# A four-layer graph network on one core: three moves of order, and the second graph's attention in the last one's buffers

## The chip, the core and the metric

The kernel runs on one core of a Trainium2 chip. The time is the device time of one execution, in microseconds. A run that is profiled is one more execution of the same program. In what follows PE is TensorE (its weight loads are shown apart as PEld), DVE is VectorE, ACT is ScalarE, POOL is GpSimd, and SP is the engine whose queue issues most of the DMAs. Every engine works through its own instructions strictly in the order in which they are written; they meet only at semaphores.

## The reference

There are 16 graphs of 1024 nodes with 128 features each, `x` (16, 1024, 128), and a matrix of integers `adj` (16, 1024, 1024) that holds 0 and 1. Four layers stand on a residual stream, and each reads a normalized copy of it:

```python
h = relu(layernorm(x));  x = x + L0(h, adj)    # degree-weighted mean, 2 batch norms
h = relu(layernorm(x));  x = x + L1(h, adj)    # graph attention
h = relu(layernorm(x));  x = x + L2(h, adj)    # attention with products as scores
h = relu(layernorm(x));  x = x + L3(h, adj)    # graph attention, elu

# L0
w = masked_row_softmax(adj.T)                  # adj is 0/1: division by the degree
region = batch_norm(w @ features @ kernel_1 + bias_1)      # over all 16 graphs
people = batch_norm(w.T @ region @ kernel_2 + bias_2)      # over all 16 graphs
# L1, and L3 with elu on the result
Wh = h @ W
e = leaky_relu(Wh @ a_src [rows] + Wh @ a_dst [columns])
out = softmax(where(adj == 0, -inf, e)) @ Wh
# L2
e = leaky_relu(sum_d hidden[i, d] * hidden[j, d] * a_0[d])  # adj == 1 only
out = softmax(where(adj == 1, e, -9e15)) @ hidden
```

Both batch norms of layer 0 need sums over all graphs, so the kernel has three stages one behind the other.

## The kernel before

Nodes are held as 8 tiles (or columns) of 128. The order of the work is written out by hand for each engine; no planner stands between.

**Stage a** (to about 252 us) walks over the 16 graphs, 8 columns c each. TensorE turns a column of `adj` (8 transposes, L360), multiplies it with the normalized x in two half-precision parts (16 matmuls, L372 to L376, into one of three PSUM banks, `psW`), and three columns later adds up sums (L335). ScalarE keeps the turned mask (`maskT`, L316) and divides column c-1 by the degree (`divide`, L296); `keep_whT` (L305) stands after column 3 and, for the column group of the graph that ended, in the next graph. VectorE has for each column the function `tail(b, c)` (L243, L245, L246: the degree and its reciprocal, which let ScalarE divide) and `rest(b, c-1)` (L251: the lower half of the quotient, which waits for ScalarE's divide and gives the PSUM bank free). I call these four instructions a pair. Between the pairs VectorE makes the next graph's normalized x: `stats` (L212), `moments` (L217, L219), then GpSimd takes a power (`rs_a`, L185), then `shifts` (L223), `normed` twice (L228), `high` (L233) and `low` (L237). TensorE waits with the next graph's first product until `low` is done. TensorE also waits, before the product of column n, until `rest` of column n-3 is done, since that is in the same PSUM bank.

**Stage b** (about 252 to 421 us) is the second half of layer 0. TensorE makes `rows(b)` (L710, 16 matmuls in the trace) and `product(b)` (L721, 32 matmuls); VectorE makes the row's parts in `graph(b)` (L620 to L636), of which L630 lets TensorE start `rows(b+1)` and L636 lets it start `product(b)`. At its start, once, `later_weights_dve` and `later_weights_pe` (L536 to L554, L533) prepare weights of stage c.

**Stage c** (421 us to the end) holds layers 1 to 3, called A, B and C, as a pipeline: the turn i works on A's attention of graph i, on B's of graph i-1 and on C's of graph i-2. In A and C the masked weights (`weights`, L1010 on VectorE, 8 tiles a graph) are the product of a row factor `row_`, a column factor `least_` and the mask from the `ring_` buffers, and TensorE's `weigh` (L1703, and L1716 in `weigh_half` where the first half of the columns is done for all tiles at once) multiplies them with `hP_`. Before that stand `columns` (L971, L974: the `peak`), `highest` on TensorE (L1653), `exponents` (L979 to L983), `rows` (L1639), then ScalarE's `exps` (L1376, L1377), `row_power` (L1384) and `factors` (L1403). In B TensorE turns the normalized values (`turn_h`, L1630 in the trace), they are split (ScalarE `g_hi`, L1445; VectorE `g_lo`, L1051), and three matmuls a tile (L1674 to L1676) make the scores. `shares` (L1032, L1034) is the reciprocal of the sums behind a weighing, `shifts` (L957) the end of a layer norm.

Of the kernel before, what the change touches and what calls it, by code (L numbers as in the profile page):

```python
# [6 lines left out]
def gnn_stack_kernel(nc, x_in, adj, k1, b1, g1, be1, k2, b2, g2, be2,  # L7
# [12 lines left out]
    P = 128  # L20
# [19 lines left out]
    with ctx:  # L40
# [84 lines left out]
        with ExitStack() as a_ctx:  # L125
# [42 lines left out]
            with nc.allow_non_contiguous_dma("small weight vectors"), nc.Block() as block:  # L168
# [38 lines left out]
                def _(dve):  # L207
# [348 lines left out]
        with ExitStack() as b_ctx:  # L556
# [16 lines left out]
            with nc.Block() as block:  # L573
# [43 lines left out]
                def _(dve):  # L617
# [86 lines left out]
                def _(pe):  # L704
# [43 lines left out]
        with ExitStack() as c_ctx:  # L748
# [37 lines left out]
            def home(x, b):  # L786

                return "A" if x == "C" and b == B - 1 else x

# [53 lines left out]
            with nc.Block() as block:  # L843
                @block.sync
                def _(sp):
# [13 lines left out]
                    def load_row(x, b):  # L859
# [3 lines left out]
                        if b > 0:  # L863
                            sp.wait_ge(S[x, "wts"], b * T)
                        sp.dma_start(row_e[x][:, :], row_dram[x][n % 2].rearrange("t p -> (t p)").partition_broadcast(P)) \
# [16 lines left out]
                    for i in range(-1, B + 2):  # L882
# [20 lines left out]
                        if 0 <= i + 1 < B:  # L903
# [38 lines left out]
                def _(dve):  # L942
# [24 lines left out]
                    def columns(x, b):  # L967
                        dve.wait_ge(S[x, "wh_made"], b + 1)
                        y = home(x, b)
                        for banks, places, tiles in GROUPS:  # L970
                            nc.vector.tensor_copy(cols[y][:, tiles, :].rearrange("p (a t) k -> p a t k", a=banks.stop - banks.start),  # L971
                                                  VALUES[y][:, banks, places, P:VW])
                        dve.drain()
                        nc.vector.reduce_max(peak[y][:, :], cols[y][:, :, 0], AXX).then_inc(S[x, "peak"], 1)  # L974

                    def exponents(x, b):
                        dve.wait_ge(S[x, "top_made"], b + 1)
                        y = home(x, b)
# [3 lines left out]
                        nc.vector.tensor_scalar(us[y][:, :], cols[y][:, :, 1], top[:, 0:1], US_MAX, ALU.add, ALU.min).then_inc(S[x, "us"], 1)  # L982
                        nc.vector.tensor_scalar(te[y][:, :], cols[y][:, :, 0], top[:, 0:1], None, ALU.subtract).then_inc(S[x, "te"], 1)  # L983

                    def lowest(x, b):
                        nc.vector.tensor_tensor(rec_top[:, 3, :], rec_top[:, 3, :], least[home(x, b)][:, :], ALU.max)

                    def factors(x, b):
                        dve.wait_ge(S[x, "exp"], b + 1)
                        y = home(x, b)  # L990
# [1339 lines left out]
```

## Time and profile before

| what | value |
|---|---|
| median of 3 runs | 1505.93 us (1505.83 to 1507.24) |
| profiled execution, its own time | 1506.49 us |
| its span from first to last instruction | 1504.7 us |
| PE busy | 1375.7 us (91%) |
| DVE busy | 1177.1 us (78%) |
| ACT busy | 818.6 us (54%) |
| POOL busy | 384.2 us (26%) |
| mean granted TensorE clock | 0.964 of full speed |

The span is divided into 40 equal slices on the profile's page; a digit is the busy share in tenths:

```
PE   5899998899946888999999999999999999999886
DVE  5788885788746668888888898888988889887565
PEclk 9999998899968989999999999999999999999998
```

TensorE is the busiest engine in every stage. Its holes are at the start, at the two borders between the stages (slices 7 and 12) and at the end. Its share of busy time says where it can't be made shorter by order alone, and the waits say where it can.

### The profile page before, as it was taken

Reading aid. Unit: us, or ns where it says so; the run is one execution under the profiler, and the core shown is the slowest. Engines: PE = TensorE matmul, PEld = TensorE weight load, DVE = VectorE, ACT = ScalarE, POOL = GpSimd, SP = SyncE. Lnnn points to the kernel's source line nnn. Section 1 sums busy time; section 2 is a strip of 40 time slices with the busy share of each in tenths; the row PEclk is TensorE's granted clock in tenths of the full one; section 3 lists DMA queues with packets and bytes.
Section 4 is the critical chain, followed back from the end, with each engine's and each line's share of the span. In section 5 each row is a group of like instructions: output and inputs, shape, how many; then the busy total and the mean of one; then the engine's idle time right before and its main releaser. Section 6 shows DMA issues by size and latency. Waiting matters only on the chain.

```text
span 1504.7 us, 33033 instructions
## 1 busy us (share of the span) xinstructions
PE 1375.7 (91%) x12642; PEld 1238.7 (82%) x12642; DVE 1177.1 (78%) x3400; ACT 818.6 (54%) x1843; POOL 384.2 (26%) x337
## 2 busy tenths in 40 slices
PE   5899998899946888999999999999999999999886
PEld 5899997555536778999999999989999889999785
DVE  5788885788746668888888898888988889887565
ACT  4788885122243564565746656556565565654621
POOL 6343430000010304314133141331423314223020
PEclk9999998899968989999999999999999999999998
DMA  9999993566612213132331432314323134132111
GB/s 206 224 226 231 223 217 130 183 241 239 208 39 76 71 41 94 50 106 83 94 93 50 113 100 71 95 51 109 106 64 99 52 104 113 44 86 56 30 43 44
DMA packets 111840, 169.36 MB, mean 113 GB/s; under 512 B 9808, under 2 KB 61760, under 8 KB 109632
## 3 DMA queue, kind: packets, MB, share of 16 engines
q1 hardware_dynamic: 87264, 125.20, 28.9%
q0 software_dynamic: 19584, 33.56, 12.3%
q10 hardware_dynamic: 4832, 8.45, 1.5%
q8 instruction: 102, 1.67, 0.4%
q14 instruction: 58, 0.48, 0.1%
HBM read 158.74 MB, written 42.00 MB: 133 GB/s over the span
## 4 chain that ended last, share of the span: by engine, by line
PE 48%; DVE 11%; DVEq 4%; ACT 3%; POOL 2%; issue 2%; ACTq 0%
PE ps L1703 31%; PE ps L1662 3%; PE ps L1685 2%; PE ps L1716 2%; PE ps L1630 2%; DVE wts_C L1010 2%; PE ps L1674 2%; PE ps L1676 2%; PE ps L1675 2%; POOL wts_B L923 1%; DVEq L1033 1%; DVE xC L1087 1%; DVE st_B L945 1%; DVE xB L1040 1%; PE ps L1639 1%
## 5 line engine op out<-in xcount | busy, mean ns | idle before, releaser
L1703 PE MATMUL ps<-hV,wts_B 128*128 128x129 f32 x2048 | 252.4, 279 | 13.0 <-POOL wts_B L923 5.2
L923 POOL TENSOR_TENSOR wts_B<-wts_B,off 128x1024 f32<-128x1024 f32 (+7 forms) x128 | 177.8, 1413 | 323.0 <-PE ps L1685 323.0
L1703 PEld LDWEIGHTS ps<-hV,wts_B 128*128 128x128 f32 x2048 | 241.3, 194 | 17.4 <-POOL wts_B L923 7.3
L1703 PE MATMUL ps<-hP_A,wts_A 128*128 128x129 f32 x1920 | 230.9, 275 | 1.1 <-ACT xB L1429 0.7
L1703 PEld LDWEIGHTS ps<-hP_A,wts_A 128*128 128x128 f32 x1920 | 221.5, 191 | 3.8 <-DVE hP_C L994 2.9
L1703 PE MATMUL ps<-hP_C,wts_C 128*128 128x129 f32 x1920 | 220.1, 274 | 0.0
L1703 PEld LDWEIGHTS ps<-hP_C,wts_C 128*128 128x128 f32 x1920 | 217.4, 191 | 0.5
L1010 DVE SCALAR_TENSOR_TENSOR wts_A<-row_A,least_A,ring_A 128x1024 f32<-128x1024 f32 x128 | 161.0, 1274 | 11.4 <-ACT row_A L1384 7.9
L1010 DVE SCALAR_TENSOR_TENSOR wts_C<-row_C,least_C,ring_C 128x1024 f32<-128x1024 f32 x120 | 166.7, 1401 | 0.0
L316 ACT ACTIVATE maskT<-ps 128x1024 fp8e4<-128x1024 bf16 x128 | 131.2, 1025 | 45.4 <-PE ps L360 33.0
L372 PE MATMUL ps<-x,adj_b 128*128 128x129 f16 x896 | 121.3, 224 | 20.9 <-DVE x L237 13.9
L1429 ACT ACTIVATE xB<-ps,rec_A 128x128 f32<-128x128 f32 x128 | 39.6, 364 | 156.0 <-DVE rec_A L1034 156.0
L373 PE MATMUL ps<-x,adj_b 128*128 128x128 f16 x896 | 121.4, 223 | 0.0
L1016 DVE SCALAR_TENSOR_TENSOR wts_B<-wts_B 128x1024 f32<-128x1024 f32 (+7 forms) x128 | 90.9, 752 | 33.6 <-ACT wts_B L1411 33.6
L372 PEld LDWEIGHTS ps<-x,adj_b 128*128 128x128 bf16 x896 | 88.2, 99 | 25.2 <-DVE x L237 16.5
L912 POOL TENSOR_TENSOR rs_C<-rs_C,mhalf 128x8 f32<-128x8 f32 x16 | 38.7, 2420 | 239.6 <-DVE rs_C L952 239.6
L721 PE MATMUL ps<-maskT,row_hi 128*128 128x512 fp8e4 x256 | 97.6, 381 | 0.0
L721 PE MATMUL ps<-maskT,row_lo 128*128 128x512 fp8e4 x256 | 97.4, 381 | 0.0
L1416 ACT ACTIVATE wts_B<-wts_B,shiftB 128x1024 f32<-128x1024 f32 (+7 forms) x128 | 89.0, 767 | 10.4 <-DVE wts_B L1016 10.0
L360 PE MATMUL ps<-ident_bf,adj_b 128*128 128x128 bf16 x1024 | 79.4, 221 | 13.5 <-DMA adj_b<-in_adj 13.5
L1411 ACT COPY wts_B<-ps 128x1024 f32<-128x1024 f32 (+7 forms) x128 | 81.0, 640 | 19.4 <-PE ps L1676 15.7
L373 PEld LDWEIGHTS ps<-x,adj_b 128*128 128x128 bf16 x896 | 88.9, 99 | 0.0
(243 smaller groups left out, 2713.7 us busy)
## 6 DMA issues: line engine op xcount, KB each, us to landing
adj_b<-in_adj POOLq DMA_DIRECT2D x120, 256.0 KB, 10.4
maskT_scratch<-maskT SPq DMA_DIRECT2D x16, 1024.0 KB, 6.8
ring_A<-maskT_scratch SPq DMA_DIRECT2D x64, 256.0 KB, 3.1
off<-maskT_scratch SPq DMA_DIRECT2D x32, 512.0 KB, 6.6
ring_C<-maskT_scratch SPq DMA_DIRECT2D x64, 256.0 KB, 3.4
xa<-in_x SPq DMA_DIRECT2D x16, 512.0 KB, 16.3
whT_b<-whT_scratch SPq DMA_DIRECT2D x16, 512.0 KB, 4.8
pTf_scratch<-pT_b SPq DMA_DIRECT2D x16, 512.0 KB, 2.9
```

The lines of the kernel that those rows point to most:

```text
L316: nc.scalar.activation(edges[:, b, c, :], psT[c % 2], ACT.Square, scale=EDGE_VALUE ** 0.5, saturate=False, accum_out=sq_all[:, n:n + 1]).t ...
L360: last = nc.tensor.transpose(psT[c % 2][:, r * P:r * P + P], adj_b[:, b % AB, r, c * P:c * P + P], ident_bf[:, :])
L372: nc.tensor.matmul(q[:, 0:GW], adj_rc, h1, start=(r == 0), stop=False)
L373: nc.tensor.matmul(q[:, 0:P], adj_rc, h2, start=False, stop=False)
L721: last = nc.tensor.matmul(psP[par][:, c * HALF:(c + 1) * HALF], part[:, par, t, :], edges[:, b, t, c * HALF:(c + 1) * HALF], start=(t == 0 ...
L923: pool.tensor_tensor(w, w, off_fp8[:, k, k * P:N], ALU.mult).then_inc(S["B", "up"], 1)
L1010: nc.vector.scalar_tensor_tensor(wts[y][:, j, :], row_e[y][:, :], least[y][:, j:j + 1], ring[x][:, j % MR, :], ALU.max, ALU.mult).then_inc ...
L1016: nc.vector.scalar_tensor_tensor(w, w, SLOPE, w, ALU.mult, ALU.max).then_inc(S["B", "lrelu"], 1)
L1411: nc.scalar.copy(wts["B"][:, j, j * P:N], P_SLOTS[j % 2][:, j * P:N]).then_inc(S["B", "kept"], 1)
L1416: nc.scalar.activation(w, w, ACT.Exp, bias=shiftB[:, 0:1]).then_inc(S["B", "exps"], 1)
L1662: last = nc.tensor.matmul(VALUES[home(x, b)][:, t // 3, t % 3, :], hT[:, t * P:t * P + P], w_use[:, cases.index(x), :], start=True, stop=True)
L1703: last = nc.tensor.matmul(Q_SLOTS[c // 2 % 2][:, c % 2, 0:PW], wts[y][:, j, c * P:c * P + P], src[:, j, :], start=(j == 0), stop=(j == T - 1))
```

## The change

The change moves instructions; it takes none away and adds none that computes.

1. In stage a, VectorE's `shifts` and first `normed` go from column 3 to column 2, the second `normed` from 4 to 3, `high` from 5 to 4 and `low` from 6 to 5.
2. In stage b, `later_weights_dve` stands behind `graph(1)`, and `later_weights_pe` behind `product(0)`.
3. In stage c, for every turn from 1 on, VectorE's `columns("A", i + 1)` stands ahead of `weights("C", i - 2, 4)`; `exponents` stay behind it.
4. In turn 0 of stage c the second graph's attention of layer A uses the buffers of C (`shelf`), which lie idle until then, so it doesn't wait for the first graph's. Its first four weight tiles go ahead on VectorE, its exponentials and factors on ScalarE, its masks on SP's queue ahead of the load of `x` 2, and TensorE weighs it (`weigh_half("A", 1)`) directly behind the first graph's and ahead of `turn_h("B", 0)`.

```diff
-                            if more and c == 3:
+                            if more and c == 2:
                                 shifts(b + 1)
-                            if more and 3 <= c < 5:
-                                normed(b + 1, c - 3)
+                            if more and 2 <= c < 4:
+                                normed(b + 1, c - 2)
+                            if more and c == 4:
+                                high(b + 1)
                             if more and c == 5:
-                                high(b + 1)
-                            if more and c == 6:
                                 low(b + 1)
...
                     graph(0, 0, True)
+                    graph(1, 1, True)
                     later_weights_dve(dve)
-                    graph(1, 1, True)
...
                     rows(0, 0, 0, True)
-                    later_weights_pe(pe)
                     rows(1, 1, 0, False)
                     product(0, 0, True)
+                    later_weights_pe(pe)
...
+            def shelf(x, b):
+
+                return "C" if x == "A" and b == 1 else home(x, b)
...
+                        if i == 0:
+                            load_mask("A", 1, 2)
+                            load_mask("A", 1, 3)
                         if 2 <= i + 2 < B:
                             load_x(i + 2)
...
-                        nc.vector.scalar_tensor_tensor(wts[y][:, j, :], row_e[y][:, :], least[y][:, j:j + 1], ring[x][:, j % MR, :],
+                        y, z = home(x, b), shelf(x, b)
+                        nc.vector.scalar_tensor_tensor(wts[z][:, j, :], row_e[z][:, :], least[z][:, j:j + 1], ring[x][:, j % MR, :],
...
                         if i == 0:
                             columns("A", 1)
                             exponents("A", 1)
+                            shares("A", 0, 2)
+                            for j in range(3):
+                                weights("A", 1, j)
+                                if j == 0:
+                                    lowest("A", 1)
...
                         if AA:
-                            shares("A", i, 2)
+                            if i > 0:
+                                shares("A", i, 2)
                             add("A", i, 0, newB, oldB)
+                        if i == 0:
+                            weights("A", 1, 3)
...
+                        if nextA and i != 0:
+                            columns("A", i + 1)
                         if CA:
                             weights("C", i - 2, 4)
                         if nextA and i != 0:
-                            columns("A", i + 1)
                             exponents("A", i + 1)
...
                         if i == 0:
-                            for j in range(2, T):
+                            for j in range(4, T):
                                 weights("A", 1, j)
...
+                            if i == 0:
+                                exps("A", 1)
                             scaled("A", i, 2)
                             if i == 0:
                                 row_power("A", 1, 0)
                                 row_power("A", 1, 1)
+                                factors("A", 1, 0)
+                                factors("A", 1, 1)
...
-                        if i in EARLY:
+                        if i == 2:
                             weigh_half("A", i)
...
+                        if i == 0:
+                            weigh_half("A", 1)
```

The kernel after has more lines ahead of these places, so its line numbers are higher: L1010 is L1019 there, L1032 is L1041, L1630 is L1653, L1639 is L1662, L1653 is L1676, L1674 is L1697, L1703 is L1726 and L1716 is L1739. Those below L780 are the same.

**VectorE in stage a.** The piece below is from one graph; `dgm`, `rdg`, `dga` and `whn` are the pair, `sf_a` is `shifts`, `xa` is `normed`. It is the place between GpSimd's power and `normed`.

```order
 L246 COPY dga<-ps 128x1
 L251 SCALAR_TENSOR_TENSOR whn<-ps,rdg,whn 128x128
-L243 TENSOR_SCALAR dgm<-ps 128x1
-L245 RECIPROCAL rdg<-dgm 128x1
-L246 COPY dga<-ps 128x1
-L251 SCALAR_TENSOR_TENSOR whn<-ps,rdg,whn 128x128
 L223 SCALAR_TENSOR_TENSOR sf_a<-mv_a,rs_a 128x8
 L228 TENSOR_SCALAR xa<-xa,rs_a,sf_a 128x128 x4
```

One pair less stands ahead of `shifts`. The same pair comes back further on, and the other end of the move is behind `low`:

```order
 L251 SCALAR_TENSOR_TENSOR whn<-ps,rdg,whn 128x128
 L237 SCALAR_TENSOR_TENSOR x<-xa,x 128x8x128
+L243 TENSOR_SCALAR dgm<-ps 128x1
+L245 RECIPROCAL rdg<-dgm 128x1
+L246 COPY dga<-ps 128x1
+L251 SCALAR_TENSOR_TENSOR whn<-ps,rdg,whn 128x128
 L243 TENSOR_SCALAR dgm<-ps 128x1
 L245 RECIPROCAL rdg<-dgm 128x1
```

`low` has one pair more behind it: column 6's, which stood ahead of it. Between `shifts` and `low` stand three pairs in both kernels.

**VectorE at the start of stage b.** `row` and `row_lo` are graph 1's row, `wsq` and `wsum` the first of the later weights.

```order
 L633 TENSOR_REDUCE r_top<-row 128x1
 L636 TENSOR_TENSOR row_lo<-row,row_hi 128x1024
+L620 COPY rdg_b<-rdeg_all 128x8
+L622 TENSOR_TENSOR row<-ps,c_rep 128x1024
+L625 TENSOR_SCALAR rdg_b<-rdg_b 128x8
+L627 TENSOR_TENSOR row<-row,rdg_b 128x1024
+L630 TENSOR_SCALAR row<-row 128x1024
+L633 TENSOR_REDUCE r_top<-row 128x1
+L636 TENSOR_TENSOR row_lo<-row,row_hi 128x1024
 L536 TENSOR_TENSOR wsq<-w3T 128x128
 L538 TENSOR_REDUCE wsum<-wsq 128x1
```

Graph 1's row now stands between graph 0's and the later weights.

**TensorE in turn 0 of stage c**, before; `wts_A` and `hP_A` are weights and values of layer A, first of graph 0 and, in the last row but one, of graph 1, `hV` is what `turn_h("B", 0)` turns:

```order
L1703 MATMUL ps<-hP_A,wts_A 128x129 x8
L1639 MATMUL ps<-ident,us_A 128x128 x4
L1703 MATMUL ps<-hP_A,wts_A 128x129 x8
L1630 MATMUL ps<-ident,hV 128x128 x8
L1716 MATMUL ps<-hP_A,wts_A 128x129 x32
L1674 MATMUL ps<-g_hi,ag_hi 128x512
```

and after, where graph 1's are in `wts_C` and `hP_C`:

```order
L1676 MATMUL ps<-ident,peak_C 128x128
L1726 MATMUL ps<-hP_A,wts_A 128x129 x8
L1662 MATMUL ps<-ident,us_C 128x128 x8
L1726 MATMUL ps<-hP_A,wts_A 128x129 x16
L1739 MATMUL ps<-hP_C,wts_C 128x129 x32
L1653 MATMUL ps<-ident,hV 128x128 x8
L1697 MATMUL ps<-g_hi,ag_hi 128x512
```

Graph 1's weighing stands ahead of the turning of `hV`, no longer behind it, and both halves of its row scores stand together.

## Rows read from the trace of the kernel before

**Rows 1.** Windows: stretch, us, PE, PEld, DVE, ACT, POOL busy, granted clock, DMA, GB/s

```profile
55.00:235.00 180.00, 168.31 (x2775) 163.70 (x2771) 147.33 (x803) 154.38 (x362) 70.81 (x105) 1.00 1.03 215
...
600.00:1400.00 800.00, 791.21 (x6762) 741.68 (x6762) 695.96 (x1765) 471.22 (x1089) 231.62 (x142) 1.00 0.30 83
```

**Rows 2.** Waits, 0 to 252 us: waiting <- awaited: total us, times, longest

```profile
DVE whn L251 <- ACT whn L296: 15.0, 18, 1.7
PE ps L372 <- DVE x L237: 13.9, 15, 2.9
```

**Rows 3.** Timeline of VectorE, one graph of stage a: start, length, operation [wait <- releaser]

```profile
69.59 0.16 DVE L243 TENSOR_SCALAR dgm<-ps 128x1 f32<-128x1 f32 x1
...
74.96 0.17 DVE L223 SCALAR_TENSOR_TENSOR sf_a<-mv_a,rs_a 128x8 f32<-128x8 f32 x1 [0.42 <-POOL rs_a L185]
...
79.28 0.15 DVE L243 TENSOR_SCALAR dgm<-ps 128x1 f32<-128x1 f32 x1
...
79.58 0.14 DVE L246 COPY dga<-ps 128x1 f32<-128x1 f32 x1
...
80.08 1.23 DVE L237 SCALAR_TENSOR_TENSOR x<-xa,x 128x1024 f16<-128x1024 f32 x1
81.22 0.15 DVE L243 TENSOR_SCALAR dgm<-ps 128x1 f32<-128x1 f32 x1
...
82.96 0.35 DVE L251 SCALAR_TENSOR_TENSOR whn<-ps,rdg,whn 128x128 f16<-128x128 f32 x1 [1.04 <-ACT whn L296]
...
83.54 0.16 DVE L243 TENSOR_SCALAR dgm<-ps 128x1 f32<-128x1 f32 x1
```

**Rows 4.** Timeline of ScalarE, the end of the same graph

```profile
80.22 0.36 ACT L296 ACTIVATE whn<-ps,rdg 128x128 f16<-128x128 f32 x1
...
82.57 0.36 ACT L296 ACTIVATE whn<-ps,rdg 128x128 f16<-128x128 f32 x1
```

**Rows 5.** Timeline of TensorE, the next graph's first matmul

```profile
81.36 0.23 PE L372 MATMUL ps<-x,adj_b 128*128 128x129 f16 x1 [0.59 <-DVE x L237]
```

**Rows 6.** Timeline of VectorE, while graph 1's x was loaded

```profile
40.95 0.87 DVE L212 BATCH_NORM_STATS2 st_a<-xa 128x6 f32<-128x128 f32 x4 [6.70 <-DMA xa<-in_x]
```

**Rows 7.** Timeline of TensorE, the start of stage b

```profile
273.76 0.59 PE L533 MATMUL ps<-w_fine,ones 128*128 128x1 f32 x2 [7.29 <-DVE w_fine L545]
274.21 3.76 PE L710 MATMUL ps<-k,whT_b 128*128 128x128 f32 x16
277.77 0.63 PE L721 MATMUL ps<-maskT,row_hi 128*128 128x512 fp8e4 x1
...
285.44 1.95 PE L710 MATMUL ps<-k,whT_b 128*128 128x128 f32 x16
```

**Rows 8.** Timeline of VectorE, the start of stage b

```profile
269.36 0.69 DVE L630 TENSOR_SCALAR row<-row 128x1024 f32<-128x1024 f32 x1
...
271.29 1.22 DVE L636 TENSOR_TENSOR row_lo<-row,row_hi 128x1024 f16<-128x1024 f32 x1
...
282.79 1.21 DVE L636 TENSOR_TENSOR row_lo<-row,row_hi 128x1024 f16<-128x1024 f32 x1
```

**Rows 9.** Waits of TensorE, 600 to 1400 us

```profile
PE ps L1653 <- DVE peak_A L974: 5.0, 11, 0.8
```

**Rows 10.** Timeline of VectorE, start of stage c

```profile
466.64 0.16 DVE L1032 TENSOR_SCALAR rec_A<-ps 128x2 f32<-128x2 f32 x1 [3.46 <-PE ps L1703]
...
476.29 3.67 DVE L1010 SCALAR_TENSOR_TENSOR wts_A<-row_A,least_A,ring_A 128x1024 f32<-128x1024 f32 x3
...
485.59 1.22 DVE L1051 TENSOR_TENSOR g_lo<-ps,g_hi 128x1024 f16<-128x1024 f32 x1
```

**Rows 11.** Timeline of TensorE, the same place

```profile
478.52 1.97 PE L1630 MATMUL ps<-ident,hV 128*128 128x128 f32 x8 [11.92 <-ACT hP_A L1403]
...
489.27 0.38 PE L1674 MATMUL ps<-g_hi,ag_hi 128*128 128x512 f16 x1
```

**Rows 12.** Granted clock in the idle stretch of TensorE

```profile
470.00:472.00 2.00, 0.00 (x0) 0.00 (x0) 0.97 (x10) 0.00 (x0) 0.80 (x1) 0.62 0.78 228
```

More of the change, by code:

```diff
@@ L902, in _ @@
                             load_mask("C", i - 1, 1)
-                        if 0 <= i + 1 < B:
+                        if 0 <= i + 1 < B and i != 0:
                             load_mask("A", i + 1, 2)
@@ L968, in columns @@
                         dve.wait_ge(S[x, "wh_made"], b + 1)
-                        y = home(x, b)
+                        y, z = home(x, b), shelf(x, b)
                         for banks, places, tiles in GROUPS:
-                            nc.vector.tensor_copy(cols[y][:, tiles, :].rearrange("p (a t) k -> p a t k", a=banks.stop - banks.start),
+                            nc.vector.tensor_copy(cols[z][:, tiles, :].rearrange("p (a t) k -> p a t k", a=banks.stop - banks.start),
                                                   VALUES[y][:, banks, places, P:VW])
@@ L992, in factors @@
                             a, t = banks.stop - banks.start, places.stop
-                            e = hP[y][:, tiles, P:PW].rearrange("p (a t) d -> p a t d", a=a)
-                            last = nc.vector.tensor_tensor(hP[y][:, tiles, 0:P].rearrange("p (a t) d -> p a t d", a=a),
+                            e = hP[z][:, tiles, P:PW].rearrange("p (a t) d -> p a t d", a=a)
+                            last = nc.vector.tensor_tensor(hP[z][:, tiles, 0:P].rearrange("p (a t) d -> p a t d", a=a),
@@ L1285, in run @@
                             weights("C", i - 2, 7)
-                        if nextA and i != 1:
+                        if nextA and i > 1 or i == -1:
                             weights("A", i + 1, 0)
@@ L1402, in factors @@
                         for t in range(h * T // 2, (h + 1) * T // 2):
-                            last = nc.scalar.mul(hP[x][:, t, 0:P], VALUES[x][:, t // 3, t % 3, 0:P], hP[x][:, t, P:PW])
+                            last = nc.scalar.mul(hP[z][:, t, 0:P], VALUES[x][:, t // 3, t % 3, 0:P], hP[z][:, t, P:PW])
                         if h == 1:
@@ L1567, in run @@
                             scaled("B", i - 1, 1)
-                        if nextA:
+                        if nextA and i != 0:
                             exps("A", i + 1)
@@ L1577, in run @@
                             scaled("B", i - 1, 2)
-                        if nextA:
+                        if nextA and i != 0:
                             factors("A", i + 1, 0)
@@ L1581, in run @@
                             scaled("B", i - 1, 3)
-                        if nextA:
+                        if nextA and i != 0:
                             factors("A", i + 1, 1)
@@ L1702, in weigh @@
                                 pe.wait_ge(S[x, "wts"], b * T + j + 1)
-                            last = nc.tensor.matmul(Q_SLOTS[c // 2 % 2][:, c % 2, 0:PW], wts[y][:, j, c * P:c * P + P], src[:, j, :],
+                            last = nc.tensor.matmul(Q_SLOTS[c // 2 % 2][:, c % 2, 0:PW], wts[z][:, j, c * P:c * P + P], src[:, j, :],
                                                     start=(j == 0), stop=(j == T - 1))
@@ L1715, in weigh_half @@
                             for c in range(T // 2):
-                                last = nc.tensor.matmul(Q_SLOTS[c // 2][:, c % 2, 0:PW], wts[y][:, j, c * P:c * P + P], hP[y][:, j, :],
+                                last = nc.tensor.matmul(Q_SLOTS[c // 2][:, c % 2, 0:PW], wts[z][:, j, c * P:c * P + P], hP[z][:, j, :],
                                                         start=(j == 0), stop=(j == T - 1))
@@ L1795, in run @@
                                     highest("A", 1, free_p, 1)
-                                if c in (5, 6):
-                                    rows("A", 1, free_p, c - 5)
+                                if c == 5:
+                                    rows("A", 1, free_p, 0)
+                                    rows("A", 1, free_p, 1)
                             if c == c0 and nextA and i > 0:
```

41 lines of the change are left out of this document (22 added, 19 removed).

## The prediction

> **What bounds the kernel now.** I read the windows of whole stages first, then the waits inside each, then the timelines of single graphs. The windows show TensorE at 168.3 of 180 us in stage a and at 791.2 of 800 us in the steady part of stage c, at a granted clock of 1.00 in both [rows 1]. So at most 8.8 us can be won in that steady stretch. In stage a 11.7 us are open, and there the other engines are nearly full too: VectorE 147.3 and ScalarE 154.4 of 180 [rows 1]. The waits of stage a say what the hole is: TensorE waits 13.9 us, once in each of 15 graphs, for VectorE's `low` (L237), and beside that VectorE itself waits 15.0 us for ScalarE's divide (L296) [rows 2]. The reader should see a ring: TensorE waits for VectorE, and VectorE for ScalarE, so an instruction that is made earlier on VectorE may make another one late that ScalarE needs. That is the question of this change, so I walk one graph by its timeline.
>
> From `tail(0)` of one graph at 69.59 to `tail(0)` of the next at 83.54 are 13.95 us [rows 3]. Ahead of `tail(0)` stands the last `rest` (82.96), which waited 1.04 us for ScalarE's last divide [rows 3]. ScalarE did that divide at 82.57, and the one of column 6 at 80.22 [rows 4]; between them stand `keep_whT` and the next graph's first mask, so the two are 2.35 us apart whatever VectorE does. The divide of column 6 needs `tail(6)`, which began at 79.28 and was through at 79.58 + 0.14 = 79.72 [rows 3].
>
> **Stage a, part 1 of the change.** It takes no instruction away. The price is in what stands between.
>
> Ahead of `shifts`: its power comes from GpSimd, and `shifts` began at 74.96 after a wait of 0.42 for it [rows 3]. The variance that GpSimd needs stays at its place. So with one pair less in the gap VectorE waits longer, and `shifts` begins at 74.96 as before, because the power isn't ready earlier. I cost that end at nothing.
>
> From `shifts` to `low` the work is the same, two `normed`, three pairs and `high`, so `low` still begins at 80.08 and the next instruction after it at 81.22 [rows 3]. TensorE began the next graph at 81.36, just behind it [rows 5]. So the wait of 13.9 us that seems to be the prize isn't shortened: what `low` waits for is the power, not its place.
>
> Behind `low`: `tail(6)` stood ahead of it, at 79.28, and now begins at 81.22, 1.94 later [rows 3]. It is through 0.44 later, at 81.66. ScalarE's divide of column 6 therefore goes from 80.22 to some 81.72 (0.06 for the semaphore), +1.50: of the 1.94, the 0.50 between 79.72 and 80.22 was slack, and the rest is passed on. From it on everything is a chain: 2.35 to the last divide [rows 4], 0.39 to the last `rest` and 0.58 to the next `tail(0)` [rows 3], so 81.72 + 2.35 + 0.39 + 0.58 = 85.04. The walk of the kernel before by the same steps gives 80.22 + 3.32 = 83.54, which is what the trace shows. The period goes from 13.95 to 15.45: **+1.50 us a graph**.
>
> TensorE also gets a wait in the middle, since the product of column 5 needs `rest(2)`, which is now behind `shifts` and the first `normed`. TensorE's own work in a period is at most 13.95 - 0.93 = 13.02 (13.9 / 15 = 0.93 is its wait) [rows 2, 3], and the new period of 15.45 has 2.4 us for it, so I cost it at nothing in the sum.
>
> How many graphs pay it: graph 15 prepares no next one. In graph 1 VectorE waited 6.70 us for x from memory [rows 6], and the first graphs are bound by such loads, so I take 12 graphs that pay in full, 18.0 us, and 0.6 for the rest: +18.6. The most is 14 x 1.50 = 21. The least, where another slack that I don't see takes it, is 0; where half of the slip hides, about +9. I take the value of the walk, since the walk meets 83.54 exactly.
>
> **Stage b, part 2.** TensorE waited 7.29 us for `w_fine` until 273.76 and began `rows(1)` at 274.21 [rows 7]. `rows(1)` itself needs L630 of graph 0, which ended at 269.36 + 0.69 = 270.05 [rows 8]. With L533 gone from ahead of it, it begins at 270.1, 4.1 earlier. `product(0)` follows 3.56 later [rows 7], at 273.7; its other condition, L636, ended at 272.51 [rows 8]. What is late next: `product(0)` itself isn't delayed. L533 stands behind it and needs the later weights, which now stand behind graph 1's L636. That one ended at 284.00 [rows 8] and goes 4.1 earlier with `rows(1)`, to 279.9; the weights took 273.76 - 272.51 = 1.25, so 281.2. `product(0)` took 285.44 - 277.77 = 7.67 [rows 7] and ends about 281.3. The two meet, and I give 0.2 for L533. **-3.9**; the most is -6 (if `rows(1)` meets a clock that has not yet fallen and takes half of its 3.56), the least 0 (if the wait comes back in full behind the product).
>
> **Steady part, part 3.** TensorE waited 5.0 us, 11 times, for `peak_A` [rows 9]. One weight tile is 3.67 / 3 = 1.22 us [rows 10]; with `columns` ahead of it `peak` comes 1.22 earlier than before, more than the longest of these waits, 0.8 [rows 9]. The 1.22 goes to the weights of C's tile 4, and they have cover: TensorE has no wait for `wts_C` beside the 5.0 us that stand at the top of that view. **-5.0**, from 0 to -5.0.
>
> **Start of stage c, part 4.** Before, TensorE stood still for 11.92 us until 478.52 and began the scores of layer B at 489.27, behind the weighing of graph 1 [rows 11]. Now this weighing stands ahead of the turning of `hV`. VectorE pays first: `shares(A, 0, 3)` at 466.64 waits behind four weight tiles and an addition. It had waited 3.46 for TensorE [rows 10], which hides part of them; I put it at about 470.5, 4 us later. The layer norm of B, and with it `hV`, comes 4 us later, at about 480.5. The last four weight tiles follow the shifts, to about 482 (4 x 1.22). Then weighing ends at 482.7, the turning (1.97 [rows 11]) begins there, and the split behind it, whose VectorE part took up the time from 485.59 (L1051 [rows 10]) to just before the scores, some 3 us or a little more: near 488.2. That is 1.1 earlier than 489.27. Against it: TensorE idles in two pieces here, and the granted clock was down to 0.62, on its way from the level of 2.4 GHz to that of 1.2, 4 us after TensorE stopped [rows 12]; so the first scores may run slow after such a gap. I take **0**, from -2 to +3. The two mask loads that SP now issues ahead of `x` 2 cost nothing, as `x` 2 is first read a turn later.
>
> The Trainium skill ("TensorE: Matmul & The Clock Gate", section "What's actually happening") says that activity releases the throttle, and the idle state is the throttled one. The row agrees, 0.62 while no matmul ran [rows 12]. By it a better filled stretch would stay fast, and part 4 would be worth about -2 rather than 0.
>
> **Sum.** +18.6 - 3.9 - 5.0 + 0 = +9.7. Against the profiled execution's 1506.49 that is 1516.2. The median of the runs is 0.56 lower, so I forecast **1515.7**.
>
> **Rivals.** *The slip hides* (the side of faster). If ScalarE's last divide is bound by its own work rather than by `tail(6)`, stage a stays and the rest remains: 1505.9 - 8.9 = 1497.0. For it: ScalarE is the fuller of the two, with 154.4 of 180 [rows 1]. Against: its mask of the next graph and the last divide follow the divide of column 6, and that one now has no slack.
> *Half of it hides*, +9 in place of +18.6: 1505.9 + 9 - 8.9 = 1506.
> *The moves do what they look like.* `low` comes a pair earlier and TensorE's 13.9 us go [rows 2], and the weighing of graph 1 fills the 11.92 us, of which 8 are won: 1505.9 - 13.9 - 8.9 - 8 = 1475.1. Against: `shifts` already waits for GpSimd [rows 3].
> *The start of stage c costs 5.* The delay of `hV` by 4 us isn't caught up, and the clock makes one more. It decides from the point where the split ends after 489.3 in the old count: 1515.7 + 5 = 1520.7. For it: the delay of 4 is certain, and what hides it is only my order of the rest.
> *The clock falls in stage a.* TensorE now pauses twice a graph, some 1.5 us each. In stage a it held 1.00 with a pause of 0.6 to 0.9 a graph [rows 1, 5]. If it fell in the most part of the columns, the 168 us of matmuls [rows 1] would become longer by up to as much again; at three quarters of it, +125: 1640. The Trainium skill names such a case (the same page, "A second HAM failure mode: psum-queue depth-cycling"): small idle gaps between groups that cycle through banks make the clock go up and down. No row of this trace shows it in stage a.
>
> **Chances.** Forecast 0.72 (its own range 1512 to 1520: stage a at +15 to +21, the other terms within 2), the slip hides 0.12, half of it 0.03, all as it looks 0.03, start of stage c 0.08, clock 0.02. Less than 0.2%, 3 us, is no change that this kernel's measurement can tell. Faster: 0.12 + 0.03 = 0.15. Same: 0.03, and 0.02 from the edge of the forecast. Slower: 0.80. The range of 8 in 10 leaves out the case at 1497, that at 1475 and that at 1640, 0.17 together: 1503 to 1523.
>
> **What would show it.** Right: VectorE's wait ahead of L223 grows from 0.42 to about 1.2, `tail(6)` follows L237 directly, the tails of two graphs are 15.4 apart, stage b begins about 18 later, and TensorE's waits for `peak_A` are gone. Stage a is wrong if the tails stay 13.95 apart; stage b is wrong if L533 waits again by more than 0.3; part 4 is wrong if the first scores of layer B (L1697), counted from the start of stage c, come more than 3 us later or more than 2 us earlier than before. The whole is wrong above all if the ring of stage a isn't the one I walked.

## The result, and the profile after

| | before | after |
|---|---|---|
| median | 1507.24 us (5 runs, 1505.83 to 1508.25) | 1515.04 us (5 runs, 1513.36 to 1518.21) |
| profiled execution | 1506.49 us | 1514.36 us |
| span | 1504.7 us | 1512.6 us |
| mean granted clock | 0.964 | 0.969 |

The ratio is 1.0057, with a 95% interval of 1.0045 to 1.007: the changed kernel is 0.6% slower. The forecast was 1515.7. That it lies within 0.7 us of the measured time is in part luck: the forecast added +9.7 to a median of 1505.93, and the measured change is +7.8 on a median that came out 1.3 us higher with five runs. In the later sets of runs the kernel before takes 1505.3 to 1505.6 us, and from there the change is +9.5.

Marks that stand in both traces show where the 7.9 us of the span come from. I take the start of the same instruction in each and subtract.

| mark | before | after | difference | step |
|---|---|---|---|---|
| last L251 of stage a | 249.32 | 269.31 | +19.99 | +20.0 |
| third `rows` of stage b | 285.44 | 300.99 | +15.55 | -4.4 |
| first `peak` of stage c | 440.47 | 456.02 | +15.55 | 0.0 |
| `peak` in turn 1 | 522.87 | 537.88 | +15.01 | -0.5 |
| moments of C, turn 3 | 603.55 | 618.26 | +14.71 | -0.3 |
| moments of C, turn 15 | 1345.08 | 1353.15 | +8.07 | -6.6 |
| end of span | 1504.7 | 1512.6 | +7.9 | -0.2 |

Stage a loses 20 us, the other moves win 12 back. This is one trace of each kernel. In the six experiments whose stage b is that of before, the way from the first mark to the second is 0.9 to 2.3 us shorter than in the trace of before, so a step of this table is good to one or two us, and the experiments below weigh more. The windows of the kernel after, with the same columns as in [rows 1]:

```profile
55.00:235.00 180.00, 155.55 (x2495) 147.37 (x2493) 131.10 (x726) 142.35 (x326) 69.32 (x104) 1.00 0.97 207
600.00:1400.00 800.00, 797.61 (x6838) 749.82 (x6837) 699.62 (x1780) 474.45 (x1098) 221.31 (x143) 1.00 0.30 84
```

In 180 us of stage a TensorE is now busy 155.6 us for 168.3, and all of VectorE, ScalarE and TensorE do less in it: the ring as a whole turns more slowly, at a clock that is still 1.00. In the steady part TensorE is at 797.6 of 800.

One graph of stage a on VectorE, after (start, length, operation, wait), for [rows 3]:

```profile
71.87 0.16 DVE L243 TENSOR_SCALAR dgm<-ps 128x1 f32<-128x1 f32 x1
...
77.23 0.17 DVE L223 SCALAR_TENSOR_TENSOR sf_a<-mv_a,rs_a 128x8 f32<-128x8 f32 x1 [1.17 <-POOL rs_a L185]
...
82.43 1.23 DVE L237 SCALAR_TENSOR_TENSOR x<-xa,x 128x1024 f16<-128x1024 f32 x1
83.57 0.15 DVE L243 TENSOR_SCALAR dgm<-ps 128x1 f32<-128x1 f32 x1
...
87.38 0.16 DVE L243 TENSOR_SCALAR dgm<-ps 128x1 f32<-128x1 f32 x1
```

ScalarE at the end of that graph, for [rows 4]:

```profile
82.73 1.02 ACT L316 ACTIVATE maskT<-ps 128x1024 fp8e4<-128x1024 bf16 x1 [0.26 <-PE ps L360]
...
84.05 0.37 ACT L296 ACTIVATE whn<-ps,rdg 128x128 f16<-128x128 f32 x1 [0.21 <-DVE dga L246]
```

And every wait of TensorE's matmuls in the graph, where [rows 5] showed only the one for `low`:

```profile
76.12 0.23 PE L372 MATMUL ps<-x,adj_b 128*128 128x129 f16 x1 [0.57 <-DVE whn L251]
...
79.27 0.23 PE L372 MATMUL ps<-x,adj_b 128*128 128x129 f16 x1 [1.37 <-DVE whn L251]
```

The period is 87.38 - 71.87 = 15.51 us; over the last 12 periods of the stage, taken from one variance (L219) to the next, it is 15.52, and 13.95 before. The wait for GpSimd ahead of L223 grew from 0.42 to 1.17, `tail(6)` stands directly behind `low`, and ScalarE's divide of column 6 comes 84.05 - 71.87 = 12.18 after `tail(0)`, for 10.63 before. All this is as the walk had it. What the walk did not have is in the first ScalarE row and the last fence: the mask of column 7, which stands ahead of that divide on ScalarE, waited for TensorE and began 82.73 - 71.87 = 10.86 after `tail(0)`. Before, the same row read:

```profile
79.21 1.02 ACT L316 ACTIVATE maskT<-ps 128x1024 fp8e4<-128x1024 bf16 x1 [0.18 <-PE ps L360]
```

That is 79.21 - 69.59 = 9.62, so the mask is 1.24 late by itself, and the divide, late by 1.55, would have been late without `tail(6)` too; `tail(6)` adds the last 0.3. TensorE had stopped twice in the middle of the graph. The first stop is for `rest(1)`, which isn't late (3.85 after `tail(0)` in both traces). The longer one, 1.37 us, is for `rest(2)`, which now stands behind `shifts` and the first `normed` and begins 7.00 after `tail(0)`, for 4.60 before.

The waits of the first 270 us (waiting, awaited, total us, times, longest), for [rows 2]:

```profile
PE ps L372 <- DVE whn L251: 32.5, 32, 4.3
```

Of the 13.9 us for `low` one wait of 2.9 us is left; the waits for `rest`, 6.8 us in 3 waits before, are 32.5 us in 32. Someone who reads only the line that was to go would call the move a success.

Stage b on TensorE, for [rows 7]:

```profile
289.54 3.75 PE L710 MATMUL ps<-k,whT_b 128*128 128x128 f32 x16 [3.73 <-DVE row L630]
300.85 0.28 PE L533 MATMUL ps<-w_fine,ones 128*128 128x1 f32 x2
```

`rows(1)` waits only for L630, 3.73 us, and L533 doesn't wait at all. The steady part's waits of TensorE, for [rows 9]:

```profile
PE ps L1726 <- POOL wts_B L932: 0.7, 1, 0.7
```

This is the longest that is left; the wait for `peak_A` is gone. At the start of stage c, for [rows 11]:

```profile
487.61 6.29 PE L1739 MATMUL ps<-hP_C,wts_C 128*128 128x129 f32 x32 [3.81 <-ACT xB L1448]
494.11 4.75 PE L1739 MATMUL ps<-hP_C,wts_C 128*128 128x129 f32 x32 [0.20 <-DVE wts_C L1019]
504.38 0.58 PE L1697 MATMUL ps<-g_hi,ag_hi 128*128 128x512 f16 x1 [4.66 <-DVE ag_lo L1063]
```

The first scores come 15.11 later than before, in a trace that was 15.55 late at the start of this stage: 0.4 won, and a new wait of 4.66 us, while the first score matmul, 0.38 us long before [rows 11], takes 0.58 here. The granted clock says why, in the windows 488 to 492 us (graph 1's weighing, behind the wait of 3.81) and 505 to 509 us (the scores, behind the wait of 4.66):

```profile
488.00:492.00 4.00, 4.00 (x20) 4.00 (x20) 2.70 (x18) 0.64 (x1) 0.98 (x1) 0.50 0.66 177
505.00:509.00 4.00, 4.00 (x11) 1.47 (x10) 0.82 (x1) 1.86 (x5) 0.00 (x0) 0.50 0.00 0
```

Both run at 0.50, the level of 1.2 GHz, each behind a stop of TensorE; in the trace of before the scores from 489 to 493 us ran at 1.00. The filled hole became two smaller ones, and behind each of them the clock was low.

### The profile page after: what moved, and what is told of

It reads as the page before. It is cut to its first block, busy times and chain, and to the rows that moved or that the text cites. A ratio compares the mean times of both kernels' runs of the same rounds, so it can differ in the third digit from the quotient of the medians.

```text
span 1512.6 us, 33032 instructions
## 1 busy us (share of the span) xinstructions
PE 1379.7 (91%) x12642; PEld 1235.9 (82%) x12642; DVE 1173.5 (78%) x3400; ACT 822.5 (54%) x1843; POOL 371.2 (25%) x337
## 4 chain that ended last, share of the span: by engine, by line
PE 55%; DVE 7%; ACT 3%; POOL 3%; DVEq 2%; issue 1%; DMA 0%; ACTq 0%
PE ps L1726 37%; PE ps L1685 4%; PE ps L1653 3%; PE ps L1708 3%; PE ps L1697 2%; PE ps L1699 2%; PE ps L1698 2%; POOL wts_B L932 1%; DVE wts_A L1019 1%; PE ps L1739 1%; PE ps L1662 1%; PE ps L1646 1%; ACT wts_B L1430 1%; DVE wts_C L1019 1%; DVEq L1042 1%
## 5 line engine op out<-in xcount | busy, mean ns | idle before, releaser
L1726 PE MATMUL ps<-hV,wts_B 128*128 128x129 f32 x2048 | 251.8, 279 | 12.4 <-POOL wts_B L932 4.6
L1726 PEld LDWEIGHTS ps<-hV,wts_B 128*128 128x128 f32 x2048 | 240.8, 194 | 17.1 <-POOL wts_B L932 6.9
L1726 PE MATMUL ps<-hP_C,wts_C 128*128 128x129 f32 x1984 | 227.9, 274 | 0.0
L1726 PEld LDWEIGHTS ps<-hP_C,wts_C 128*128 128x128 f32 x1984 | 224.9, 191 | 0.5
L1726 PE MATMUL ps<-hP_A,wts_A 128*128 128x129 f32 x1856 | 222.9, 275 | 1.2 <-ACT xB L1448 0.7
L1726 PEld LDWEIGHTS ps<-hP_A,wts_A 128*128 128x128 f32 x1856 | 214.0, 191 | 3.8 <-DVE hP_C L1003 2.9
L1019 DVE SCALAR_TENSOR_TENSOR wts_C<-row_C,least_C,ring_C 128x1024 f32<-128x1024 f32 x120 | 166.7, 1401 | 0.0
L1019 DVE SCALAR_TENSOR_TENSOR wts_A<-row_A,least_A,ring_A 128x1024 f32<-128x1024 f32 x120 | 151.1, 1275 | 8.8 <-ACT row_A L1402 7.9
L372 PE MATMUL ps<-x,adj_b 128*128 128x129 f16 x896 | 121.5, 224 | 36.1 <-DVE whn L251 32.5
```

What stands on the lines that cost most here:

```text
L372: nc.tensor.matmul(q[:, 0:GW], adj_rc, h1, start=(r == 0), stop=False)
L1019: nc.vector.scalar_tensor_tensor(wts[z][:, j, :], row_e[z][:, :], least[z][:, j:j + 1], ring[x][:, j % MR, :], ALU.max, ALU.mult).then_inc ...
L1726: last = nc.tensor.matmul(Q_SLOTS[c // 2 % 2][:, c % 2, 0:PW], wts[z][:, j, c * P:c * P + P], src[:, j, :], start=(j == 0), stop=(j == T - 1))
```

## The experiments

All are timed over five rounds. The median of the kernel before was 1505.6, 1505.3 and 1505.5 us in the three sets on their chips; each time below is compared with its own set.

**e1, stage a's move undone.** The four terms seemed separate in the ledger.

```diff
-                            if more and c == 2:
+                            if more and c == 3:
                                 shifts(b + 1)
...
-                            if more and c == 5:
+                            if more and c == 6:
                                 low(b + 1)
```

> The changed kernel with the move in stage a alone undone (shifts at column 3 again, low at 6). The ledger of the two traces reads: stage a +19.8, start of stage b -4.2, start of stage c -0.9, steady part -6.6 us. If these four are separate, this kernel takes 1507.2 - 4.2 - 0.9 - 6.6 = 1495.5 us. Rival: what TensorE gains later is only what it lost in stage a (a transfer or buffer that had to catch up), then undoing stage a's move gives 1505 to 1507.

1496.46 us (1495.55 to 1496.60), ratio 0.9938 [0.9924, 0.9952]. Moves 2 to 4 alone make the kernel 0.6% faster, and the rival (1505 to 1507) is out. The agreement with 1495.5 flatters: that sum started from 1507.2, and against its own set, 1505.6, this kernel gains 9.1 us where the ledger's terms make 11.7. In its trace the start of stage c, from the first `peak` to turn 3, is 1.8 us longer than before, for 0.8 shorter in the changed kernel. So the terms are separate to 2 or 3 us.

**e2, stage a's move alone**, on the kernel before; the diff is the first hunk of the change.

> The kernel before with the move in stage a alone. Separate parts: +19.8, so 1527. Rival (part of the loss is made good later, or belongs to another part): under 1520.

1525.46 us (1523.07 to 1526.86), ratio 1.013 [1.0115, 1.0146]: +19.9. The period is 15.52, as in the kernel after. So the loss is this move's and no other's.

**e3 and e4, the move in two halves.** The trace left two reasons: a late `tail(6)`, my step, and a late `rest(2)`, which I had put at nothing. The front half moves only `shifts` and `normed`, the back half only `high` and `low`:

```diff
+++ e3, front
-                            if more and c == 3:
+                            if more and c == 2:
                                 shifts(b + 1)
-                            if more and 3 <= c < 5:
-                                normed(b + 1, c - 3)
+                            if more and 2 <= c < 4:
+                                normed(b + 1, c - 2)
+++ e4, back
-                            if more and c == 5:
+                            if more and c == 4:
                                 high(b + 1)
-                            if more and c == 6:
+                            if more and c == 5:
                                 low(b + 1)
```

> The kernel before with only the front of stage a's move: shifts and the first normed at column 2, the second normed at 3; high and low stay at columns 5 and 6. tail(6) stays ahead of low, rest(2) goes behind shifts and the first normed. Theory 1 (the step of the prediction: the late tail(6) holds up ScalarE's divides): tail(6) isn't late, only low is, by one pair, 0.6 us: +0.6 a graph at most, +0 to +7 us. Theory 2 (rest(2) is late, TensorE's column 5 waits for its bank, 1.2 us later in the graph than before, and everything behind it on TensorE and ScalarE follows): +1.2 to +1.8 a graph, +14 to +22 us.

1519.78 us (1518.93 to 1520.70), +14.2, period 15.21, which is +1.26 a graph. Theory 1 allowed at most 7 us, so it falls for this half; theory 2 holds, at its lower end. TensorE stops for `rest(2)` in the middle, and at the end of the graph ScalarE's mask of column 7 waits for TensorE, with the divide of column 6 directly behind it:

```profile
109.11 0.23 PE L372 MATMUL ps<-x,adj_b 128*128 128x129 f16 x1 [1.06 <-DVE whn L251]
...
112.57 1.02 ACT L316 ACTIVATE maskT<-ps 128x1024 fp8e4<-128x1024 bf16 x1 [0.27 <-PE ps L360]
...
113.58 0.36 ACT L296 ACTIVATE whn<-ps,rdg 128x128 f16<-128x128 f32 x1
```

`tail(0)` of this graph began at 101.71, so the mask comes 10.86 behind it, as in the kernel after, and the divide 11.87, which is 1.24 more than before: nearly the 1.26 of the period. The move also makes `tail(3)` and `tail(4)` late for ScalarE (its waits for L246, these among them, are 19.5 us between 55 and 235 us, 2.4 before). That is a rival for the same loss, but the mask of column 7 waited for TensorE all the same, so TensorE's way is the longer. No run moves `rest(2)` alone.

> The kernel before with only the back of stage a's move: shifts and normed stay at columns 3, 3 and 4, high goes to 4 and low to 5. tail(6) goes behind low, rest(2) stays where it was. Theory 1: low begins one pair (0.62 us) earlier, tail(6) begins 1.94 - 0.62 = 1.32 later, less 0.50 of slack and with 0.06: +0.88 a graph, +10 to +12 us. Theory 2: nothing is late in the middle, 0, or down to -0.6 a graph as low is earlier: -8 to +1 us.

1514.82 us (1513.90 to 1517.52), +9.2, period 14.87, +0.92 a graph, for the 0.88 worked out. Here theory 2 falls and theory 1 holds. ScalarE waits for `tail(6)`'s result in the row that it predicted, and the next divide is 2.36 later:

```profile
111.44 0.37 ACT L296 ACTIVATE whn<-ps,rdg 128x128 f16<-128x128 f32 x1 [0.57 <-DVE dga L246]
...
113.80 0.36 ACT L296 ACTIVATE whn<-ps,rdg 128x128 f16<-128x128 f32 x1
```

Both theories are true, each of its half. Together the halves cost 1.57 a graph and not 1.26 + 0.92 = 2.18: they delay the same divide by two ways, and the later one counts. By TensorE alone it comes 11.87 after `tail(0)` (e3), by `tail(6)` 12.18 (the kernel after).

**e5, `tail(6)` ahead of `low` again**, on e4; this changes nothing but the place of three instructions (L243, L245, L246).

```diff
-                            tail(b, c)
+                            if not (more and c == 6):
+                                tail(b, c)
...
                             if more and c == 5:
+                                tail(b, 6)
                                 low(b + 1)
```

> The back half of stage a's move on the kernel before (high at column 4, low at 5), with tail(6) alone put ahead of low again; rest(5) stays behind it. If the late tail(6) is what the back half costs (+9.2 us measured, period 14.87 for 13.95), the period falls to 13.9 to 14.0 and the time to that of before within 3 us. Rival: the back half costs by rest(5), which the next graph's first product needs (it is as late here as there): the period stays over 14.6 and the time over 1512.

1508.34 us (1506.18 to 1509.79), ratio 1.0019 [1.001, 1.0028]: +3.1, period 14.17. Most of the back half's loss, 0.70 of 0.92 a graph, is `tail(6)`; the rest is not, and `rest(5)`, which is still late, is the nearest cause that the waits show (10.9 us of TensorE on L251 between 55 and 235 us, 1.1 before); no run moves it alone. The theory is right in its direction and missed both of its bounds by a little (13.9 to 14.0, and 3 us).

**e6, the moments a pair earlier**, on e1: if the power from GpSimd is what `low` waits for, then give GpSimd its input earlier.

```diff
-                            if more and c < 2:
-                                stats(b + 1, c)
-                            if more and c == 1:
+                            if more and c == 0:
+                                stats(b + 1, 0)
+                                stats(b + 1, 1)
                                 moments(b + 1)
```

> On the best so far (stage a's move undone, 1496.5): both halves of the statistics and the moments of the next x at column 0, ahead of tail(1) and rest(0). The variance comes one pair (0.6 us) earlier, so GpSimd's power and low do, while tail(1) is 1.8 us later against a slack of ScalarE of some 1.2. Theory (low is what binds TensorE in the order of before, everything else has a little slack): -0.3 to -0.6 a graph, 1489 to 1493. Rival (the ring of tails binds: ScalarE's divide of column 1 gets late): 0 or up to +0.6 a graph, 1496 to 1504.

1504.98 us (1502.62 to 1507.06), 8.5 more than e1, period 14.62. A miss, outside the ranges of the theory and of its rival: `tail(1)` is now what is late, and ScalarE's divide of column 1 waits for it (1.28 us in the graph at 102 us). It is the same ring, entered at another column, and again what came too late cost more than what came earlier gave.

**e7, `columns` alone**, on the kernel before; the diff is that of the change.

> The kernel before with part 3 alone (columns ahead of the weights of C's tile 4). By the shift of the peaks in the changed kernel it gives 11 turns of 0.6 us: 1505.6 - 6.6 = 1499.0. By the waits of TensorE's matmuls as the prediction summed them, 5.0: 1500.6. Rival: the gain in the changed kernel came from the start of stage c (another phase between the graphs), then under 2 us.

1498.64 us (1497.49 to 1499.38), ratio 0.9957 [0.9944, 0.9971], -6.65. In its trace the moments of C come 2.41 us earlier than before in turn 3 and 9.05 in turn 15, so 6.64 are won between the two, 0.6 in each of 11 turns, as in the kernel after. The view that gave 5.0 is that of the matmuls; the same view of the tile `peak_A` before has a row for the weight load, which is late by more (total us, times, over the whole trace):

```profile
  PEld ps L1653: 7.6, 12
  PE ps L1653: 5.7, 12
```

7.6 / 12 = 0.63 a turn, and 11 turns are 6.9: what this wait costs was nearer to the weight load's row than to the matmul's. The rival of the start of stage c, under 2 us, is out.

**e8, the turning of `hV` behind six tiles**, on e1.

```diff
                         if i == 0:
-                            weigh_half("A", 1)
+                            weigh_half("A", 1, range(0, 6))
+                            turn_h("B", i, hV[i % 2], free_p, 0, "lo")
+                            weigh_half("A", 1, range(6, T))
```

> On the best so far (1496.5): in turn 0 the turning of hV for layer B stands behind the first six tiles of graph 1's weighing, not behind all eight. hV is ready 2.6 us before the turning begins in the changed kernel, so the turning begins about 2.5 earlier, the split ends 2.5 earlier, and TensorE's pause ahead of the first scores is 3.0 us and no longer 4.7, so these may run at the full clock (they took 0.43 us apiece for 0.21 at first). Theory (the filling's gain was lost to the turning's place and to the clock): -2.5 to -5, 1491.5 to 1494. Rival (the first scores don't bind the turn): 0.

1493.67 us (1492.62 to 1495.19), 2.8 less than e1. TensorE's wait ahead of the first scores is 2.88 and no longer 4.66, and the first score matmul takes 0.38 us again:

```profile
482.31 0.38 PE L1697 MATMUL ps<-g_hi,ag_hi 128*128 128x512 f16 x1 [2.88 <-DVE ag_lo L1063]
```

From 484.65 us on matmuls of the same shape take 0.63 us, and the granted clock from 484 to 486 us is 0.50, so it still falls, only later. The first scores come 2.8 us earlier than in the kernel before, counted from the first `peak`, where the kernel after and e1 won 0.4. So a part of the filling's gain had gone here: it filled the hole and pushed the chain behind it.

**e9, the fourth weight tile into VectorE's wait**, on e8.

```diff
-                        if i == 0:
-                            weights("A", 1, 3)
...
                             moments("B")
+                        if i == 0:
+                            weights("A", 1, 3)
```

> On the kernel at 1493.7 (stage a undone, turning of hV behind six tiles): in turn 0 the fourth weight tile of graph 1 goes from ahead of shares(A, 0, 3) to behind the moments of layer B, where VectorE waits 1.75 us for GpSimd. shares(A, 0, 3) comes at about the end of the third tile, 1.7 us earlier; TensorE's wait of 3.8 us and ScalarE's of 4.0 us ahead of their next work both end on it. Theory (hV's chain binds the first scores): -1.7, 1492.0. Rival (the last four weight tiles or the ring of masks bind): 0.

1492.14 us (1490.07 to 1493.63), 1.5 less than e8, with ranges that overlap. The size agrees, but the traces don't bear the theory out. TensorE's wait ahead of graph 1's weighing fell from 3.81 to 2.61 us, but new waits of 0.22 and 1.73 us for `wts_C` took it back, and the first scores, counted from the first `peak`, come only 0.2 us earlier than in e8. Most of the 1.6 us between the two traces stands in the last turns, where the same 116 matmuls of `wts_B` take 14.57 us in e9 and 16.08 in e8, at a granted clock of 0.79 (1425 to 1433 us) and 0.60 (1426 to 1434). The move itself is worth about 0.2 us by this, and the agreement with -1.7 is luck.

**e12, the copies of the degrees ahead of the last `rest`**, on e9.

```diff
-                        rest(b, T - 1)
+                        dve.drain()
                         nc.vector.tensor_copy(rdeg_all[:, b * T:b * T + T], rdg[:, :])
                         nc.vector.tensor_copy(deg_all[:, b * T:b * T + T], dga[:, :])
                         dve.drain()
+                        rest(b, T - 1)
```

> The kernel of e9 and, in stage a, the two small copies of the degrees ahead of the last rest of a graph, in the microsecond in which VectorE waits for ScalarE's last divide, not behind it. tail(0) of the next graph comes 0.3 us earlier. If tail(0) is in the ring that sets the period: -0.3 in some 13 graphs, -4 us against e9, period 13.65. If the period is set by TensorE's wait for low and the end of TensorE's column alone, with tail(0) having slack: 0.

1489.34 us (1487.49 to 1490.73), ratio to before 0.9895 [0.988, 0.9911]: the fastest kernel here, 1.1% faster than before. But the period in its profile is 13.99, not 13.65 (13.93 in e9). Single periods are down to 13.50, and others are longer, up to 15.02, where VectorE waits for x from memory (wait, 45 to 250 us, for 1.3 us in 3 waits before):

```profile
DVE st_a L212 <- DMA xa<-in_x: 4.4, 6, 1.1
```

So the theory isn't borne out. That the move works within a graph and the loads take it back would fit, but no run changes the loads, and e9 has a period of 13.60 too. Where the 2.8 us of its median come from is not settled: in the one profile of each its stage a ends 0.7 us later than e9's, and the gain stands behind that, 1.9 us to the third `rows` of stage b and 1.9 from turn 1 to turn 3 of stage c, where the two kernels have the same instructions.

**e10, part 2 alone**, and **e11, part 4 alone**, on the kernel before, with the diffs of the change.

> The kernel before with part 2 alone (later weights behind graph 1 and product 0). By the ledger -4.2 to -4.4: 1501.0. The prediction's term: -3.9.

1501.79 us (1499.33 to 1503.98), ratio 0.9977 [0.9969, 0.9986], -3.7.

> The kernel before with part 4 alone (the second graph's attention in C's buffers, its first tiles and its weighing ahead). By the ledger of the changed kernel -0.5 to -0.9 us, by the one with stage a undone +0.9: 1504.4 to 1506.5, no change that can be told. The prediction's term: 0, from -2 to +3. The rival of the prediction: +5.

1506.22 us (1504.17 to 1507.92), ratio 1.0003 [0.9994, 1.0011]: no change that can be told. The prediction's rival of +5 is out. In its trace the way from the first `peak` to turn 3 is 2.3 us longer than before, as it was 1.8 longer in e1 and 0.8 shorter in the kernel after. So what part 4 does there is known to some 3 us, and why the three differ is open; the granted clock falls at other places in each of them.

The single parts add up: +19.9 - 3.7 - 6.6 + 0.7 = +10.3 for +7.8 measured in one piece, or for the +9.5 that it makes against the medians of the later sets. That is 2.5 or 0.8 us apart, with four uncertainties of about 1 to 2 us in the sum.

## Why the prediction was right, step by step

- **Stage a, +18.6.** Measured +20.0 in the trace and +19.9 alone. The period was to go from 13.95 to 15.45 and went to 15.52. That `shifts` gains nothing (5.37 after `tail(0)` before, 5.36 after) and that `low` isn't earlier (10.49 and 10.56) stand in the traces, and that the late `tail(6)` goes through ScalarE to the next graph is shown by e4 (+0.92 for +0.88) and e5. One step was wrong: "TensorE also gets a wait in the middle ... so I cost it at nothing". e3, which has this wait and no late `tail(6)`, costs 1.26 a graph. My reason was that the new period has room for TensorE's work. It has room for the work, but TensorE's masks feed ScalarE at a certain column, and what counts is when they come, not whether all fit in the period. The sum was right because both ways lead to the same divide and the later one counts, and the way that I walked is the later one, by 0.3 us (12.18 against 11.87 after `tail(0)`). That is luck, since I hadn't walked the other. For the front half alone the same reasoning gave 0 to 7, and it was 14.
- **How many graphs pay.** 18.6 / 1.50 = 12.4 were taken; 20.0 / 1.57 = 12.7.
- **Stage b, -3.9.** -4.4 in the ledger, -3.7 alone; the second is the better measure, since the trace of before is 0.9 to 2.3 us slow on this stretch. `rows(1)` waits for L630 and for nothing else, and L533 waits no more.
- **Steady part, -5.0.** -6.6, in the trace and alone: the term that was most mis-sized. The mechanism is the one named; the wait was to be read at the weight load (0.63 a turn) and not at the matmul (0.45).
- **Start of stage c, 0.** -0.8 in the ledger to turn 3, +0.7 alone with an interval around no change. The delay of `hV` is as named (4.3 us, counted from the first `peak`), and the first scores ran at a granted clock of 0.50, as feared. The thought that a better filled stretch stays fast didn't come true here: the weighing and the scores each began behind a new stop, of 3.81 and 4.66 us, and ran at 0.50. That the turning waited for the last tiles of the weighing was in the working, and e8 shows that it was a place to win 2.8. The single traces put this term between -0.8 and +2.3, so the 0 is met no more closely than that.
- **The rival "the slip hides"** (1497.0) fell: ScalarE had 0.5 of slack and no more (e4's 0.92 is 1.32 less the slack, within 0.1). Its number is nearly that of e1, where the slip doesn't exist. **The clock** stayed at 1.00 in stage a with two pauses a graph, one of them 1.4 us.

## What to carry to other kernels

Where engines form a ring, an instruction that is put earlier makes those that it passes later, and if they feed another engine, their price is read at that engine: when does it need them, and how much slack did it have (here 0.5 us of 1.94). This has to be walked for each engine that is fed: here a second way, through TensorE, was within 0.3 us of the one that was walked. The line of the waits that is to go doesn't tell whether the thing awaited can come earlier; look at what that waits for in its turn (here GpSimd's power). And when a hole is filled, look at who stood behind the hole in the same queue: filling the 11.9 us gained nothing that could be told until the waiting chain's one step was let past the filling.

## What the runs showed of the hardware that I had not expected

A short wait of TensorE for a matmul whose weights come from the awaited tile costs 0.60 us a turn where the matmul's row shows 0.45 and the weight load's 0.63. Weight loads do not keep strictly to the order of the matmuls in time: PEld is busy 741.7 us beside PE's 791.2 in 800 [rows 1], so most loads run under a matmul. The load of `peak_A` takes 0.13 us (the median of its 17 in the trace of before), which is about what the matmul's row leaves out. That this load can't run ahead, because it waits for the tile itself, and so comes on top is my reading; no run tests it. The weight load's row isn't the price everywhere: in the same stretch loads for the scores of B wait 19.1 us for `wts_B`, of which TensorE's matmuls show nothing.

In stage a the loads may not be far from binding: in the trace of e12, with single periods down to 13.50 us, x arrives late by up to 1.1 us, and in the kernel before the DMA engines' share is 1.03 at a period of 13.95 [rows 1], for 0.97 at 15.52 after. No run changes the loads, so this is a guess from the waits: in orders much faster than 13.9 us a graph I would look at the loads next.
